# An image's result stored before its last term is added, and the last term added to it in DRAM by a transfer

## The reference, cut to what matters

```python
x = x + _L0_conv_ref(_gn(x), ...)     # mixture of experts, a 1x1 convolution
x = x + _L1_conv_ref(_gn(x), ...)     # depthwise 3x3, then 1x1
x = x + _L2_conv_ref(_gn(x), ...)     # attention over the 784 pixels
x = x + _L3_conv_ref(_gn(x), 0)       # box mean: each tap 1/9, padding 1
```

## Time and profile before

| | |
|---|---|
| median of 3 runs | 1625.53 us |
| profiled execution | 1624.92 us |
| its span in the trace | 1623.1 us (1.8 us less than its time) |
| granted TensorE clock, mean | 0.973 |
| TensorE matmuls busy | 1530.0 us (94%) |
| VectorE busy | 1376.0 us (85%) |
| ScalarE busy | 1362.3 us (84%) |
| GpSimd busy | 189.1 us (12%) |
| bytes read and written in HBM | 29.29 MB and 25.69 MB |

### The profile page before, as it was taken

The page is one execution under the profiler, slowest core; times in us unless marked ns, Lnnn a source line. Parts: engine busy times, 40 slices in busy tenths (PEclk is TensorE's granted clock), DMA queues, the critical chain, the costliest instruction groups (busy, mean ns, idle before and its releaser), DMA issues. The chain is left out here.

```text
span 1623.1 us, 26428 instructions
## 1 busy us (share of the span) xinstructions
PE 1530.0 (94%) x8190; PEld 1149.4 (71%) x8190; DVE 1376.0 (85%) x2466; ACT 1362.3 (84%) x3496; POOL 189.1 (12%) x142
## 2 busy tenths in 40 slices
PE   4469999999999999999999999999999999999993
PEld 2247777777777777777777777777777777776773
DVE  5877689999888998988889998888999988888446
ACT  3368998988999888899998889999888899987862
POOL 1111011011110101111011111101101111010000
PEclk8689999999999999999999999999999999999996
DMA  4000011000111110011111001111100011000001
GB/s 148 20 20 21 21 40 41 31 29 22 40 40 40 40 40 20 20 40 40 40 40 40 20 20 40 40 40 40 40 27 28 24 40 40 21 21 21 21 20 40
DMA packets 21058, 55.58 MB, mean 34 GB/s; under 512 B 2321, under 2 KB 3345, under 8 KB 21010
## 3 DMA queue, kind: packets, MB, share of 16 engines
q1 hardware_dynamic: 20914, 54.98, 9.6%
q10 hardware_dynamic: 96, 0.00, 0.0%
HBM read 29.29 MB, written 25.69 MB: 34 GB/s over the span
## 5 line engine op out<-in xcount | busy, mean ns | idle before, releaser
L770 DVE SCALAR_TENSOR_TENSOR h<-xpad,dw_sb,h 128x784 f32<-128x784 f32 x512 | 495.9, 1031 | 0.0
L541 PE MATMUL tile_ps<-wqk,xn_parts 128*112 128x512 f32 x1344 | 363.8, 425 | 0.0
L541 PEld LDWEIGHTS tile_ps<-wqk,xn_parts 128*112 128x112 f32 x1344 | 235.3, 175 | 79.6
L583 PE MATMUL tile_ps<-k,xT 112*128 112x256 f32 x896 | 205.2, 388 | 7.7 <-ACT xT L1026 7.7
L583 PEld LDWEIGHTS tile_ps<-k,xT 112*128 112x128 f32 x896 | 174.3, 195 | 40.2 <-issue 8.4
L449 PE MATMUL conv_ps<-h,pw_masked 128*128 128x392 f32 x512 | 180.5, 496 | 5.5 <-issue 5.5
L960 ACT ACTIVATE junk<-x 128x784 bf16<-128x784 f32 x192 | 162.3, 848 | 23.6 <-DVE x L797 15.5
L571 PE MATMUL conv_ps<-x,mixed 128*128 128x392 f32 (+1 forms) x512 | 175.1, 494 | 2.2 <-ACT mixed L994 1.1
L1234 POOL TENSOR_SCALAR pw_masked<-pw_sb,hmask 128x256 f32<-128x256 f32 x64 | 119.1, 1869 | 433.9 <-DVE hmask L778 425.5
L1221 POOL TENSOR_SCALAR xpad<-x,gn_r,gn_s 128x784 f32<-128x784 f32 x64 | 64.4, 1013 | 894.2 <-DVE gn_s L701 894.2
L449 PE MATMUL conv_ps<-xn_parts,w_out 128*128 128x392 f32 x768 | 152.7, 347 | 0.0
(11 more groups left out here) (138 smaller groups left out, 2646.9 us busy)
## 6 DMA issues: line engine op xcount, KB each, us to landing
x<-x SPq DMA_DIRECT2D x32, 784.0 KB, 4.3
out<-x SPq DMA_DIRECT2D x32, 784.0 KB, 3.4
expert_sb<-expert_rows SPq DMA_DIRECT2D x8, 256.0 KB, 5.2
x<-w_qk SPq DMA_DIRECT2D x1, 512.0 KB
x<-w_vT SPq DMA_DIRECT2D x1, 256.0 KB
x<-w_ln SPq DMA_DIRECT2D x1, 256.0 KB
pw_sb<-pw_wT SPq DMA_DIRECT2D x1, 256.0 KB
gmean<-group_mean SPq DMA_DIRECT2D x1, 64.0 KB, 3.8
```

The costliest lines, as they stand in the source:

```text
L541: mm = nc.tensor.matmul(bank, xn2_parts[:, u, i, m * TOK:(m + 1) * TOK], wqk[:, v, i, :], start=False, stop=(i == J - 1 and u == 1))
L583: mm = nc.tensor.matmul(tile_ps[:, KX_BANK, i * C:(i + 1) * C], xT[:, m, half(i)], k2[:, m, :], start=(m == 0), stop=(m == M - 1))
L770: ins = nc.vector.scalar_tensor_tensor(acc, view, scalar, acc, ALU.mult, ALU.add)
```

## The change

The sum x4 is no longer made in SBUF. SyncE stores x3 of image t-4 in the step in which it is made. The 1/9 goes into the scale and shift of the last group norm (`box_scale`, a new VectorE instruction on 128 x 4 elements, right behind `scales_shifts`, from which `normalise_x3` reads). The fourth box addition writes to a tile of its own, `boxed`, with one buffer. GpSimd's queue then issues one transfer from `boxed` to the output in DRAM that adds to what is there (`accum_op=ALU.add`), after the wait for the box sum and for the store of x3. `make_x4` is gone. `gn_r` and `gn_s` become the two halves of one tile `gn_rs`.

```diff
@@ box_operands
-                    (inner, inner, row_sums[:, :, 2:2 + H, :])][n]
+                    (boxed[:].rearrange("p j (h w) -> p j h w", w=W), inner, row_sums[:, :, 2:2 + H, :])][n]
@@ SyncE
             def step(t):
-                Z, F = t + 1, t - 5
+                Z, E = t + 1, t - 4
...
-                if F.active:
-                    sp.wait_ge(x4_ready.sem, x4_ready.at(F))
-                    sp.dma_start(out_dram[F.times(1)], x3[:, F.odd]).then_inc(stored.of(F), 16)
+                if E.active:
+                    sp.wait_ge(x3_ready.sem, x3_ready.at(E))
+                    hold(sp, "sp")
+                    sp.dma_start(out_dram[E.times(1)], x3[:, E.odd]).then_inc(stored.of(E), 16)
 
             run(sp, step)
             for last in (Image(None, IMAGES - 2), Image(None, IMAGES - 1)):
                 sp.wait_ge(stored.of(last), stored.at(last))
+                sp.wait_ge(boxed_added.of(last), boxed_added.at(last))
@@ VectorE
+            def box_scale(A, F):
+
+                dve.wait_ge(gn.sem, gn.at(A))
+                if (F - 1).active:
+                    dve.wait_ge(x3pad_ready.sem, x3pad_ready.at(F - 1))
+                nc.vector.tensor_scalar(box_rs[:], gn_rs[:, :, 3, :], 1.0 / TAPS, None, ALU.mult).then_inc(box_scaled.sem, 1)
...
             def make_x3(E):
                 if (E - 2).active:
                     dve.wait_ge(stored.of(E - 2), stored.at(E - 2))
+                    dve.wait_ge(x3pad_ready.sem, x3pad_ready.at(E - 2))
...
                         dve.wait_ge(box_step.sem, box_step.at(F, n))
+                    if n == BOX_STEPS - 1 and (F - 1).active:
+                        dve.wait_ge(boxed_added.of(F - 1), boxed_added.at(F - 1))
                     dst, a, b = box_operands(n)
                     nc.vector.tensor_tensor(dst, a, b, ALU.add).then_inc(box_step.sem, 1)
-
-            def make_x4(F):
-                dve.wait_ge(box_step.sem, box_step.at(F))
-                for j in range(J):
-                    x4 = x3[:, F.odd, j, :].rearrange("p (h w) -> p h w", w=W)
-                    nc.vector.scalar_tensor_tensor(x4, x3pad[:, j, 1:1 + H, 1:1 + W], 1.0 / TAPS, x4, ALU.mult,
-                                                   ALU.add).then_inc(x4_ready.sem, 1)
...
                     scales_shifts(A)
+                if F.active:
+                    box_scale(A, F)
                 if E.active:
                     kx_low(E)
...
-                if F.active:
-                    make_x4(F)
@@ ScalarE
-            def normalise_x3(A, F):
+            def normalise_x3(F):
 
                 if (F - 1).active:
-                    act.wait_ge(x4_ready.sem, x4_ready.at(F - 1))
-                normalise(A, 3, [x3pad[:, j, 1:1 + H, 1:1 + W] for j in range(J)],
-                          [x3[:, F.odd, j, :].rearrange("p (h w) -> p h w", w=W) for j in range(J)], x3pad_ready)
+                    act.wait_ge(box_step.sem, box_step.at(F - 1))
+                act.wait_ge(box_scaled.sem, box_scaled.at(F))
+                for j in range(J):
+                    nc.scalar.activation(x3pad[:, j, 1:1 + H, 1:1 + W], x3[:, F.odd, j, :].rearrange("p (h w) -> p h w", w=W),
+                                         ACT.Identity, bias=box_rs[:, 1, j:j + 1],
+                                         scale=box_rs[:, 0, j:j + 1]).then_inc(x3pad_ready.sem, 1)
@@ GpSimd
+            def add_boxed(F):
+
+                pool.wait_ge(box_step.sem, box_step.at(F))
+                pool.wait_ge(stored.of(F), stored.at(F))
+                hold(pool, "pool")
+                pool.dma_start(out_dram[F.times(1)], boxed[:], accum_op=ALU.add).then_inc(boxed_added.of(F), 16)
...
                 if C_.active:
                     mask_weights(C_)
+                if F.active:
+                    add_boxed(F)
```

More of the change, by code:

```diff
@@ L170, in build @@
         row_sums = sb("row_sums", [P, J, PH, W])
+        boxed = sb("boxed", [P, J, HW])
         wqk_raw = x3[:, 0].rearrange("p j n -> p (j n)")[:, 0:J * 2 * C].rearrange("p (j n) -> p j n", j=J)
@@ L185, in build @@
         gn_sd = sb("gn_sd", [P, 4, J])
-        gn_r = sb("gn_r", [P, 4, J])
-        gn_s = sb("gn_s", [P, 4, J])
+        gn_rs = sb("gn_rs", [P, 2, 4, J])
+        gn_r, gn_s = gn_rs[:, 0], gn_rs[:, 1]
+        box_rs = sb("box_rs", [P, 2, J])
         pooled = sb("pooled", [P, 2, J])
@@ L235, in build @@
         stored = DmaCount([sem("stored_even"), sem("stored_odd")])
+        boxed_added = DmaCount([sem("boxed_added_even"), sem("boxed_added_odd")])
         gn = sig("gn", GN_DONE)
@@ L291, in build @@
         x3pad_ready = sig("x3pad_ready", J)
+        box_scaled = sig("box_scaled")
         box_step = sig("box_step", BOX_STEPS)
-        x4_ready = sig("x4_ready", J)
         x_dram = x.rearrange("b (j p) h w -> b p j (h w)", p=P)
@@ L698, in scales_shifts @@
                 dve.wait_ge(gn_sqrt.sem, gn_sqrt.at(A))
-                nc.vector.reciprocal(gn_r[:], gn_sd[:]).then_inc(gn.sem, 1)
+                nc.vector.reciprocal(gn_r, gn_sd[:]).then_inc(gn.sem, 1)
                 dve.wait_ge(gn.sem, gn.at(A, GN_R))
-                nc.vector.scalar_tensor_tensor(gn_s[:], gn_avg[:, :, 0:2], -1.0, gn_r[:], ALU.mult,
+                nc.vector.scalar_tensor_tensor(gn_s, gn_avg[:, :, 0:2], -1.0, gn_r, ALU.mult,
                                                ALU.mult).then_inc(gn.sem, 1)
+            def box_scale(A, F):
[3 more added lines that the diff above has]
+                nc.vector.tensor_scalar(box_rs[:], gn_rs[:, :, 3, :], 1.0 / TAPS, None, ALU.mult).then_inc(box_scaled.sem, 1)
             def gate_logits(A):
@@ L1154, in step @@
                 if F.active:
-                    normalise_x3(A, F)
+                    normalise_x3(F)
                 if C_.active:
```

## The result

The changed kernel takes 1631.9 us (median of 7 runs, 1628.73 to 1633.15), against 1626.7 for seven runs of the kernel before. The ratio is 1.0037, with a 95% interval of 1.0022 to 1.0053: 3.6 to 8.6 us slower, which is clear of the noise, and by about 0.4%, still within the 0.5% that stood for "no change". The forecast was 1626.5, range 1618 to 1645, with "no change" the likeliest. The profiled execution took 1632.63 us (span 1631.0); that of before took 1624.92 (span 1623.1).

The account below looks back on a forecast made before the run. TensorE's own work was taken as some 46.8 us a step, with a dependence loop through other engines 0.2 us longer. 1624.92 - 3.72 + 0.20 + 1.35 + 3.16 = 1625.9 us, or 1626.5 against the median; range 1618 to 1645.

Parts of the forecast that it names:

- The main reading: Steady steps: the VectorE time freed by make_x4 becomes waiting for ScalarE; gain 0.
- What bounds the kernel, and the worth of `make_x4`: TensorE and a dependence loop bound the steps; dropping make_x4 gains 0 there, 3.72 us at the end.
- `box_scale`: Between gn_s and kx_low: 0.05 us a step, 0 to 0.17 possible; 0.20 us in the last step.
- The steady step: Loop of 27 steps: 1.35 us added in all, ends 0 and 4.6, all from box_scale; step still 47.0 us.
- Store a step earlier, fourth addition into `boxed`: SyncE's x3 store about 810.9 us delays no load; the box addition keeps shape and size; cost 0.
- The end: After the last addition: issue 1.0 plus landing 6.0, 7.0 us (ends 3.8 and 9.7), 3.16 more than before.
- The wait of the fourth addition of image 31: Near the kernel's end: image 30's transfer has 8.95 us before this wait costs anything; taken as 0.
- the issue pushing the taps: VectorE's taps behind the box sums, slowed by GpSimd's issue: 13 us at three pushes a step, 30 at seven; chance 0.25.
- The long transfer: Adding transfer of 12 us from issue to landing: end pays 5.0 and an earlier wait 3.05 more, 1634.6; chance 0.07.
- VectorE as the bound: Steady steps: modelled matmul times hide VectorE as limit, so 27 x 1.86 = 50 us go, about 1576; chance 0.04.

Follow-up runs that it names:

- e3: The kernel before with box_scale alone added, make_x4 kept and no transfer from GpSimd; 1630.6 us, ratio 1.0031.
- e8: The changed kernel with box_scale behind the second pair of q_low calls and the last image's sum made in SBUF; 1626.62 us, ratio 1.0001.
- e5: The changed kernel with the adding transfer issued as two, one for each half of the channels; 1631.66 us in one run.
- e4: The kernel before with make_x4 left out and nothing put in its place; 1622.56 us, ratio 0.998.
- e12: The kernel before with two short ScalarE operations exchanged, kx_high ahead of mean_columns; 1620.91 us, ratio 0.9975.
- e2: The changed kernel with box_scale moved one place only, behind kx_low and ahead of the gate chain; 1630.89 us in one run.

## Why the prediction was right

The measured 1631.9 us lie in the range, and within 0.5% of the point estimate; the sum was 5 us short. The main reading, that VectorE's freed time is worth nothing in a steady step, was right, and it decides the outcome. That the rest stayed this small is in part luck: the range reached to 1645 for pushes that don't occur, and what came instead, a collision in the loop and two waits at the end, was at nothing in the sum. Point by point:

- **What bounds the kernel, and the worth of `make_x4`:** right. Its time became the wait of `ymask` for ScalarE, at the 1.6 us forecast, and left out alone it gave 3.3 us, all at the end, where 3.72 were forecast. VectorE's busy time fell by 47 us where about 60 was the sign.
- **`box_scale`:** right in place, bounds and size. The cover was the 0.16 us in which VectorE waits for ScalarE. It hides the operation in one of the loop's two steps and not in the other, where `kx_low` is 0.09 us late in the changed kernel: 0.045 us a step on average, for the 0.05 taken. Added alone to the kernel before it costs twice that (e3).
- **The steady step:** this is the term that failed. The sum had 1.35 us for 27 steps; they cost 3.5, of which `box_scale` is some 1.2 (27 x 0.045). The other 2.3 are a term that it put at nothing: a collision between instructions that were both there before, the second `pooled` operation and GpSimd's second `xpad`. That operation then takes 0.95 instead of 0.2 us, which delays `q_low` by 0.2 us and makes the step 0.1 to 0.2 us longer (e8). The forecast had looked for disturbance between GpSimd and VectorE at the new issue, and there it is zero (e5), while the rows of the old pair (L708 at 0.47 and L713 at 0.72 us, for 2 and 16 elements) were read and not priced. What tips it isn't known. By the recorded starts, `pooled` comes 50 to 55 ns behind GpSimd's second instruction in the kernels that never collide (before, e4, e12) and 38 to 49 ns behind it in those with a transfer (outside e2), in colliding and in other steps alike. Why kernels with a transfer on GpSimd's queue fall on the wrong side in 15 to 27 of 32 steps, one with two transfers in 1, and the four without in none, stays open.
- **Store a step earlier, fourth addition into `boxed`:** cost 0, right. x3's store at 814.50 us, 811.2 on the clock of the step before the change, delayed no load (842.24, as far behind `xpad` as before).
- **The end:** the step that failed beside it. I took 7.0 us from the last addition to the end, with 9.7 as the upper bound; it is 9.8. Issue and landing were 1.0 and 6.0 in the sum, and from the start of the issue to the landing it is 7.2, so that part was right, though by a wrong reading: the landing time of the earlier trace rows counts from the start of the issue, and the issue was put on top of it. What the sum had at nothing are the waits on both sides. 1.0 us passes between the addition's end and the issue, where SyncE needs 0.03. Behind the landing 1.6 us pass, where a store by SyncE leaves 0.44, because GpSimd's own closing instruction ends last. The wait of the fourth addition of image 31 stayed free with one transfer; with two halves it showed, with 0.19 us (e5).
- **The rivals:** the issue pushing the taps, at 0.25 my dearest, is excluded. The long transfer (12 us) didn't come: it is 7.2, near the sum's 7.0. VectorE as the bound is excluded by e4.
- **Sum of the profiled executions:** +3.5 in the steps, -1.7 for the x4 of image 30 with `box_scale`, +4.0 at the end (9.8 for 5.8) make +5.8, near the 5.2 between the medians. The other 2 us of the 7.9 lie in the first steps and the last but one, where the clock scatters. Whether any of that belongs to the change stays open: `xpad` of image 4 starts between 187.4 and 189.6 us in the seven profiles with GpSimd's transfers and no further wait, between 186.5 and 188.0 in the four without.

## What to carry to other kernels

Before giving a freed engine credit, look what it waits for next: here nearly all of VectorE's 54 us turned into waits for ScalarE, and only what lay at the end of the kernel was worth anything. An adding transfer took twice the time of a store (7.1 against 3.4 us), and issued by GpSimd it had 1.0 us ahead of it and 1.6 behind it. In the steps that was hidden, at the end of the kernel it was not, and making the last image's sum in SBUF took 4 us off that end in the trace, 3.1 by the ratios of whole runs. Read what a time is counted from before you add to it. And where a loop of waits through other engines ran 0.2 us longer than the busiest engine's own work, the order of short operations on that loop was the cheapest gain; one exchange of two ScalarE operations was worth more than the whole change.

## What the runs showed of the hardware that I had not expected

A VectorE operation on 2 elements with two inputs in SBUF can take 0.95 us, the rest of a GpSimd instruction beside it, to 0.01 us. The Trainium skill (SBUF — State Buffer, Who interferes with whom) says of such a pair that the one that comes second waits until the first is done, and the trace agrees for the steps that collide: 850.63 against 850.62. In the steps that don't, the operation also starts some 0.04 to 0.05 us behind GpSimd's second instruction by the recorded starts, and is done in 0.21 us. So these starts don't tell which of the two came first. A collision made the step 0.1 to 0.2 us longer.

A transfer issued by GpSimd occupied it for 0.76 us when plain and 1.2 us when adding. Its issue started 0.6 to 1.0 us behind the VectorE operation that it waited for, while SyncE's started within 0.1 us (1620.09 + 1.86 to 1621.98). When such a transfer was the kernel's last, 1.6 us passed between its landing and the end, adding or plain, and 2.9 with two of them, against 0.44 behind a store by SyncE.

Runs of one kernel spread over 6 us in step with the mean granted clock: of the kernel before from 1621.67 at 0.976 to 1627.94 at 0.969. The stretches at half clock (1.2 GHz) lie only in the first 120 us and behind 1450 us. A single profile therefore can't carry a difference of 2 us in those stages. Inside the steady steps it can: the kernel before and e4, which differ there only in work that is hidden, have their 20 steps within 0.3 us of each other.
